# Zero rows of a routing buffer written in 16 KB pieces per partition instead of single 512-byte rows

## What is computed

```
x = L0_attn_x                                   # (2, 1024, 128), float32
# layer 0: RWKV-6 linear attention (2 heads of 64), then top-1 of 16 experts, 256 wide, gelu
h = layernorm(x) * (1 + ca) + sa;  x = x + ga * rwkv6(h)
h = layernorm(x) * (1 + cb) + sb
assign = argmax(h @ router_w);  w = sigmoid(logit of assign)
x = x + gb * w * (gelu(h @ w1[assign] + b1[assign]) @ w2[assign] + b2[assign])
# layer 1: higher-order linear attention (16 heads of 32), then top-2 of 4 live experts, 704 wide, silu
h = layernorm(x) * (1 + ca') + sa';  x = x + ga' * hla(h)
h = layernorm(x) * (1 + cb') + sb'
x = x + gb' * sum over 2 experts of weight_e * (silu(h @ w1_e) * (h @ w3_e)) @ w2_e
```

## Time and profile before

| what | us |
|---|---|
| median of 3 runs | 737.74 |
| the runs | 732.66, 738.21, 737.74 |
| the profiled execution, first to last instruction | 735.5 |
| its PE, busy | 672.1 (91%) |
| its DVE, busy | 431.7 (59%) |
| its ACT, busy | 291.5 (40%) |
| its POOL, busy | 261.0 (35%) |

### The profile page before, as it was taken

The page is one execution under the profiler, slowest core; times in us unless marked ns, Lnnn a source line. Parts: engine busy times, 40 slices in busy tenths (PEclk is TensorE's granted clock), DMA queues, the critical chain, the costliest instruction groups (busy, mean ns, idle before and its releaser), DMA issues.

```text
span 735.5 us, 26532 instructions
## 1 busy us (share of the span) xinstructions
PE 672.1 (91%) x10978; PEld 571.0 (78%) x10978; DVE 431.7 (59%) x1382; ACT 291.5 (40%) x971; POOL 261.0 (35%) x399
## 2 busy tenths in 40 slices
PE   5798887989977987799999999999999899999995
PEld 4466555766767986688888888888887798999995
DVE  3776775787632423356777768676766554444443
ACT  1443443444201531345455455454544343333321
POOL 2353553445750002112434433344423332232225
PEclk9677997799875999799999999999999999999998
DMA  6999999100002651000000000000040355767462
GB/s 185 303 285 329 294 284 272 26 3 8 24 22 79 177 152 46 9 4 11 11 16 14 15 18 12 22 8 22 11 147 10 117 196 207 229 210 250 170 229 58
DMA packets 83687, 82.48 MB, mean 112 GB/s; under 512 B 5600, under 2 KB 73408, under 8 KB 80624
## 3 DMA queue, kind: packets, MB, share of 16 engines
q1 hardware_dynamic: 78192, 74.00, 32.9%
q0 software_dynamic: 2912, 6.03, 2.5%
q10 hardware_dynamic: 2464, 0.76, 0.5%
HBM read 49.45 MB, written 35.64 MB: 116 GB/s over the span
## 4 chain that ended last, share of the span: by engine, by line
PE 55%; DVE 2%; DMA 1%; issue 1%; ACT 0%; POOL 0%; SPq 0%; DVEq 0%; POOLq 0%
PE bank L1900 6%; PE quad L1758 6%; PE quad L1882 5%; PE quad L1884 5%; PE bank L1783 4%; PE pair L1720 3%; PE bank L1807 3%; PE quad L1764 2%; PE pair L1722 2%; PE pair L1721 2%; PE bank L1820 2%; PE bank L1823 2%; PE pair L1745 2%; PE bank L1810 2%; PE bank L1902 1%; PE quad L1887 1%
## 5 line engine op out<-in xcount | busy, mean ns | idle before, releaser
L2157 DVE TENSOR_TENSOR h_masked<-quad,const 128x1536 f32<-128x1536 f32 (+2 forms) x66 | 112.6, 1705 | 58.1 <-PE quad L1764 48.6
L1994 ACT ACTIVATE f_sa<-quad 128x256 f32<-128x256 f32 (+1 forms) x115 | 40.1, 351 | 93.6 <-PE quad L1884 76.0
L2271 DVE TENSOR_TENSOR f_hid<-f_sa,quad 128x256 f32<-128x256 f32 (+1 forms) x115 | 43.0, 379 | 52.2 <-ACT f_sa L1994 52.1
L1882 PE MATMUL quad<-f_xT,wall 128*128 128x256 f32 (+1 forms) x190 | 50.9, 350 | 2.8 <-DVE f_hid L2271 2.7
L1900 PE MATMUL bank<-wall,f_hid 128*128 128x128 f32 x390 | 50.7, 277 | 1.1 <-DVE f_hid L2274 0.9
L1900 PEld LDWEIGHTS bank<-wall,f_hid 128*128 128x128 f32 x390 | 47.8, 192 | 3.6 <-DVE f_hid L2274 2.8
L1884 PE MATMUL quad<-f_xT,wall 128*128 128x256 f32 (+1 forms) x190 | 49.7, 343 | 0.0
L1758 PE MATMUL quad<-h_qk 32*128 32x128 f32 x1024 | 47.0, 298 | 0.0
L2380 POOL DMA_INDIRECT moe_slots<-g_pay,g_slot x28 | 28.3, 1010 | 42.2 <-DVE g_pay L2125 30.4
L777 POOL TENSOR_TENSOR kl<-kl,tot 128x128 f32<-128x128 f32 x56 | 25.1, 448 | 51.0 <-DVE state L676 20.7
L1971 ACT ACTIVATE h_gT<-bank 128x128 f32<-128x128 f32 x64 | 17.7, 277 | 63.9 <-PE bank L1810 63.9
(11 more groups left out here) (415 smaller groups left out, 1874.8 us busy)
## 6 DMA issues: line engine op xcount, KB each, us to landing
wall<-moe_w SPq DMA_DIRECT2D x23, 1088.0 KB, 5.2
moe_slots<-blank SPq DMA_DIRECT2D x16, 1024.0 KB, 9.8
moe_slots<-blank SPq DMA_DIRECT2D x2, 2112.0 KB, 19.3
wall<-in_experts_dram SPq DMA_DIRECT2D x1, 4120.0 KB, 20.7
e_w<-in_experts_dram SPq DMA_DIRECT2D x15, 257.5 KB, 2.9
moe_slots<-blank SPq DMA_DIRECT2D x1, 1984.0 KB, 13.8
moe_slots<-e_yg SPq DMA_DIRECT2D x7, 256.0 KB, 2.8
f_xg<-moe_slots SPq DMA_DIRECT2D x12, 132.0 KB, 4.2
```

What stands on the lines that cost most here:

```text
L1882: pe.matmul(up_bank(n, f)[:, 0:s], w[:, F1 + TAIL1 + f * P:F1 + TAIL1 + (f + 1) * P], x_of(n)[:, 0:s], start=True, stop=True)
L1994: act.activation(sa[g % 3][:, 0:s], up_bank(n, f)[:, 0:s], ACT.Silu).then_inc(f_sa, 1)
L2157: dve.tensor_tensor(masked[k % 4][:, :, a * P:z * P], quad[:, :, a * P:z * P], cst("causal")[:, None, a * P:z * P].to_broadcast([P, HPG, ( ...
L2271: dve.tensor_tensor(hid[n % 2][:, f, 0:s], sa[g % 3][:, 0:s], up_bank(n, f)[:, T1:T1 + s], ALU.mult)\
```

## The change

The zero rows come from a tile `zeros` of 128 partitions by 4096 float32 (16 KB in each partition), which POOL sets once after `mix(0)`. Each partition writes 32 neighbouring rows of one expert's region as one piece of 16 KB; the eight partitions that belong to one expert cover the 256 rows of a slab. A slab is one DMA of 2 MB, where it was two of 1 MB. The rows behind the regions go in pieces of 31 rows. SP waits for POOL's memset (`s_set` at 4) before the first of them, and POOL's waits count one DMA for each slab. The bytes written are the same.

```diff
+RUN = 2 * E0
...
+        zeros = sb("zeros", [P, RUN * C])
...
-            regions = t["moe0_slots"][0:E0 * REGION, :].rearrange("(e s k p) n -> s k p e n", e=E0, k=2, p=P)
+            sp.wait_ge(s_set, 4)
+            regions = t["moe0_slots"][0:E0 * REGION, :].rearrange("(e s u r) n -> s e u (r n)", e=E0, u=P // E0, r=RUN)
             for g, slabs in enumerate(SLABS):
                 for s in slabs:
-                    for k in range(2):
-                        sp.dma_start(regions[s, k], blank[:, 0:1, 0:C].to_broadcast([P, E0, C])).then_inc(s_slab[g], 16)
+                    sp.dma_start(regions[s], zeros[:, :]).then_inc(s_slab[g], 16)
                 if g == 1:
                     sp.dma_start(wall[:, :, :], t["experts0"].rearrange("e p n -> p e n")).then_inc(s_wall, 16)
-            sp.dma_start(t["moe0_slots"][E0 * REGION:, :].rearrange("(q p) n -> p q n", p=P),
-                         blank[:, 0:1, 0:C].to_broadcast([P, 2 * EXTRA0 + 1, C])).then_inc(s_slab[len(SLABS) - 1], 16)
+            sp.dma_start(t["moe0_slots"][E0 * REGION:, :].rearrange("(p r) n -> p (r n)", p=P),
+                         zeros[:, 0:(2 * EXTRA0 + 1) * C]).then_inc(s_slab[len(SLABS) - 1], 16)
...
                 mix(0)
+                pool.memset(zeros[:, :], 0.0).then_inc(s_set, 1)
...
-                        pool.wait_ge(s_slab[g], 16 * (2 * len(slabs) + (g == len(SLABS) - 1)))
+                        pool.wait_ge(s_slab[g], 16 * (len(slabs) + (g == len(SLABS) - 1)))
```

## The result

The changed kernel takes 738.57 us in the median of 20 runs (731.26 to 744.98), the kernel before 733.31 in 20 runs beside it (725.68 to 738.21). The ratio is 1.0063, with a 95% interval from 1.0038 to 1.0087: slower by 0.6%, 4.6 us at the measured ratio. The forecast was 731.5. Each kernel's runs lie up to 14 us apart; one profile shows one draw from such a spread. The profiled execution of the changed kernel took 740.48, its span 738.3. Ratios compare fast runs alone (a run over 1.5% above the fastest of its kernel is left out), so they needn't equal the ratio of two medians.

A forecast was written before the change was run, and what follows sets the result against it. It took PE's program fetches queued behind full DMA traffic, not the zeros, as the cost. Terms 0 + 0 + 0 - 6.2 + 0 on 735.5 gave 729.3, plus 2.2 for the median 731.5; range 726 to 749, likeliest case 729 to 734.

The forecast's parts named there:

- The fourth stop: PE's 3.60 us wait before 121.21 goes because traffic ends at 110; step 4 becomes 21.3 us: -6.2.
- SP's wait: SP's wait for the memset before the zero writes: SP arrives 8.5 us after the memset's end, cost 0.
- The memset: POOL's new memset behind `mix(0)`: at most 5.0 us, ending at 26.1, cost 0; upper bound +3.5.
- Rate and end of the traffic: Zero writes and the 2.0 MB behind them: 400 GB/s, 47 us, ending at 110 instead of about 129.
- The first three stops: PE's waits before 56.92, 79.97 and 100.43: fetches queue behind 60 to 85 KB, 2.4 to 3.4 us; change 0.
- What such a stop costs: PE's fetch stops: 1.5 to 1.8 us absorbed in steps 2 and 3; at most 9.6 us blamed on traffic altogether.
- The -6.2: Gain in step 4, 27.47 us in the profile, when its 3.60 us stop and the clock fall behind it go.
- rival (b): DMA queue turns go by pieces: 48 pieces pass ahead of a fetch, PE stops some 17 us; 755, chance 0.18.
- Rival (c): Writes to places 1 MB apart run at 200 GB/s; traffic ends at 157, step 5 gets a stop; 744, chance 0.08.
- The mild form of (b): Only the slab in progress lies ahead of a fetch, up to 5.3 us; two stops cost 1 to 3 us more.
- (a): Nothing measurable: traffic not fast enough, or the clock falls in another step; 736 to 739, chance 0.24.

The follow-up runs named there:

- serial 1 MB (8 KB spread, 512 bytes): Two kernels, SP waiting for each 1 MB DMA: 8 KB pieces over spread rows with memset, ratio 0.9889; the kernel before's 512-byte pieces without memset, 0.9920.
- all serial: The one-in-flight kernel with 1 MB DMAs of 8 KB pieces, plus a wait behind each of nine copies into `moe1_w` ahead of the zeros; ratio 0.9960.
- portions: The changed kernel's 16 KB pieces, with SP waiting before each portion of transfers until PE finished a step's leaf products; ratio 1.0027.
- memset alone: The kernel before plus POOL's memset of the 16 KB tile and SP's wait, zeros still written in 512-byte pieces from the old tile; ratio 1.003.
- serial with neighbouring rows: The one-in-flight kernel with 1 MB DMAs of 8 KB pieces, each DMA writing one expert's 2048 neighbouring rows instead of spread rows; ratio 0.9905.
- 16 KB over neighbouring rows: The changed kernel, each 2 MB DMA writing 4096 neighbouring rows instead of 256 rows in each of 16 regions; ratio 0.9965.
- before again: The kernel before, unedited, profiled a second time; 740.72 us in its one execution.
- changed again: The changed kernel, unedited, timed and profiled again on a second chip beside the kernel before; ratio 1.0052.
- 512 bytes in 2 MB: The changed kernel's eight 2 MB slab DMAs, but in 512-byte pieces, each over 4096 neighbouring rows; ratio 1.0042.
- 8 KB in 1 MB: The changed kernel with each slab written by two 1 MB DMAs in 8 KB pieces instead of one 2 MB DMA in 16 KB pieces; ratio 0.9969.
- serial 16 KB in 2 MB: The one-in-flight kernel with the changed kernel's 2 MB slabs of 16 KB pieces instead of 1 MB DMAs of 8 KB; ratio 1.0138.

## Why the prediction was wrong

Its frame held. Nobody waits for the zeros: the gain of the transfer by itself is 0. The full DMA engines act on PE through its program fetches. The fourth stop went. That step 4 then took 21.36, forecast 21.3, is luck: the forecast wanted a clock near 1.00 and it was 0.84, low without any stop. In the second profile of the changed kernel the same step had 1.00 and took 18.8; so step 5 was the wrong measure of an undisturbed step. SP's wait is free. The memset ended at 24.6, under the bound of 26.1. POOL's first `kl` product moved by 1.15 us and the second by 0.31; the second waits for DVE, one of whose instructions right behind the memset was 0.30 us longer. Rate and end of the traffic were half right: 399 GB/s behind the `wall` load, forecast 400, but 256 ahead of it. It ended near 122, not at 110, and that was still early enough for the fourth stop.

The step that failed is "The first three stops": "If what lies ahead is 60 to 85 KB, it is 4 to 5 of the new pieces", and with it the waits of 2.4 to 3.4 us and the term of 0. Behind the second stop 138 KB lay ahead, 5.3 us. Neither pieces nor bytes were the right measure. Over the kernels what lay ahead of a fetch was 97 to 164 pieces of 512 bytes in 1 MB DMAs, 169 in 2 MB DMAs, 14 of 8 KB, 9 of 16 KB in spread rows and 6 of 16 KB in neighbouring ones. At this place bytes and time go from 59 KB and 3.3 us before to 138 KB and 5.3 us after, with 117 and 90 KB and 4.4 and 3.6 us for the 8 KB pieces and the neighbouring rows. The term was +8.8 on the profiled steps 1 to 3 in place of 0, against the -6.1 gained in step 4: +2.65. The stops themselves grew by 3.9 us of the 8.8; most of the rest is the low clock behind them, taken up below.

The two stretches that the prediction read the earlier trace rows were also the wrong ones. They precede fetches that came in time. Counting PE's instructions, the stops stand 512 apart (248 matmuls, 247 weight loads and 17 of its sequencer from the first to the second), and the fetch that ends a stop is the one behind the block change in the middle. For the second stop that change is at 73.80 us before and at 77.27 after; the queue up to the fetch, from 73.8 to 77.5 us before and from 77.3 to 82.4 after:

```profile
q1 hardware_dynamic: 2286, 1.16, 105.2%
...
q1 hardware_dynamic: 139, 2.02, 98.5%
```

The fetch began 3.7 us behind the change before and 5.2 us after. PE ran through the block in 4.5 us in both, and resumed 2.4 and 2.3 us behind the start of the fetch; that gives stops of 1.6 and 3.0, and the profile has 1.45 and 2.71. The same wait grew from 4.3 to 6.0 us for the first stop. For the third it was 7.1 before, with 125 KB ahead on an engine, and 7.0 after; its stop grew because PE ran through the block 0.6 us faster and resumed 0.4 us later behind the fetch. At the second place all fourteen profiles line up:

| profiles | wait of the fetch behind the block change, us | stop, us |
|---|---|---|
| serial 1 MB (8 KB spread, 512 bytes), all serial, portions, memset alone | 1.3 to 2.0 | none |
| serial with neighbouring rows, before | 3.7, 3.7 | 1.34, 1.45 |
| 16 KB over neighbouring rows | 4.1 | 1.86 |
| before again, changed again, 512 bytes in 2 MB, 8 KB in 1 MB | 4.5 to 4.8 | 2.1 to 2.4 |
| changed | 5.2 | 2.71 |
| serial 16 KB in 2 MB | 7.0 | 4.86 |

"What such a stop costs" was wrong as well: "In steps 2 and 3 a stop of 1.5 to 1.8 us is absorbed". These steps took 20.5 us at a clock of 1.00 with their stops; the kernel before profiled again has a step without stop, in full traffic and at 1.00, that took 18.7. The stop cost about its own length.

To the stop itself comes the clock. From 45 to 130 us all profiles together have twenty stops of 1.86 us or more, and behind each the granted clock fell to 0.50 (or had just done so), for 3 to 17 us. Of the nine from 0.7 to 1.8 us, two did (1.66 and 1.50; 1.45 and 1.78 did not). The clock fell without a stop too: step 2 of the serial 1 MB kernel has none, a clock of 0.84 and 21.8 us, 3 more than the steps at 1.00 beside it. So a stop isn't the only cause of a low clock, and either costs without the other. Steps without stop and at 1.00 took 18.7 to 19.1; so the kernel before was already paying in steps 1 to 4, 91.8 and 87.5 us in its two profiles, where the four serial kernels with 1 MB DMAs need 77 to 79. One profile isn't enough to see it: that of memset and wait alone has 79.7. The runs of one transfer in flight test this cause from both sides: little ahead of a fetch, 0.4 to 1.1% faster than before; much ahead, 1.4% slower.

A second error was the base. The -6.2 was read off one profiled execution, with a fourth stop of 3.6 us and a step of 27.5. The second profile has the same stop and a step of 24.9, the one of memset and wait alone neither. The median of before stood at 737.74 in 3 runs and is 733.31 in 20, 4.4 us less. The rival (b), that a turn goes by pieces, isn't what happened: 48 pieces didn't pass ahead of a fetch, only 9. The Trainium skill ("DMA: Bandwidth & Descriptors", section "Queues, rings and completion order") has turns of up to 64 descriptors. The traces show neither that many with 16 KB pieces nor that few with 512-byte ones, 97 to 164. The other rule of the Trainium skill, on a row pitch that is a large power of two (the same page, section "Latency and other measured facts"), was given too little weight. Spread rows moved at 256 GB/s as a stream and 211 alone, neighbouring ones at 415, and this layout costs about 0.9% between two kernels that otherwise do the same. Rival (c) named it, but as a threat by a later end of the traffic; it acted by longer waits instead. The mild form of (b) was closest: its 5.3 us ahead of a fetch is what was measured. It was given 1 to 3 us on two stops; three stops grew by 1.8, 1.3 and 0.8, and their steps by 3 each. That 738.57 lies in the span of (a) is luck: the traffic did get faster.

## What to carry to other kernels

A transfer that nobody waits for can still cost, because the engines' programs come through the same DMA engines: look for waits on "issue" under full DMA, and for the instruction queue's packets around them. What gained here is less in flight. Faster bytes alone, in neighbouring rows, took the loss away and gave no clear gain. A wait of SP behind each background DMA of about 1 MB gained 0.8 to 1.1% in three kernels here (0.4% in a fourth), with pieces of 512 bytes as with 8 KB, while 2 MB DMAs in 16 KB pieces to regions 1 MB apart lost, as a stream (0.6%) and one at a time (1.4%). Before an effect of 1% is read from a profile, two or three profiles of the same kernel show which of its waits are there each time.

## What the hardware showed that wasn't expected

- The stops stand two program blocks apart, 247 matmuls and 248 weight loads. The Trainium skill ("Runtime: NRT & Kernel Launch", section "Instruction fetch mechanics") calls the cost of crossing a block mostly hidden; under full DMA these traces have four stops of 1.5 to 3.6 us before and three of 2.6 to 3.5 after.
- Sixteen engines that write 16 KB pieces to regions 1 MB apart ran at 211 GB/s for one 2 MB DMA alone, at 256 in the first slabs of a stream and at 399 in those behind the `wall` load. The same pieces in one block ran at 415 to 427.
- DVE's second L465 (L463 before), at 24.65 us just behind the memset's end and beside POOL's first `kl` product, took 0.99 us. In the kernel before, where that product was over, and in the second profile of the changed one, where it came later, it took 0.69.
